# Second cross attention of a two-layer block: keys projected once per batch instead of folded into the queries

## What is computed

```python
def _L1_xattn_ref(q, k, v, Wq, bq, Wk, bk, Wv, bv, Wo, bo):
    HEADS = 16; D_MODEL = 128; D_K = D_MODEL // HEADS
    qh = (q @ Wq + bq).reshape(B, LQ, HEADS, D_K).transpose(0, 2, 1, 3)
    kh = (k @ Wk + bk).reshape(B, LKV, HEADS, D_K).transpose(0, 2, 1, 3)
    vh = (v @ Wv + bv).reshape(B, LKV, HEADS, D_K).transpose(0, 2, 1, 3)
    attn = jax.nn.softmax(jnp.einsum('bhqd,bhkd->bhqk', qh, kh) / np.sqrt(D_K), axis=-1)
    out = jnp.einsum('bhqk,bhkd->bhqd', attn, vh)
    return out.transpose(0, 2, 1, 3).reshape(B, LQ, D_MODEL) @ Wo + bo
```

## Time and profile before

| | |
|---|---|
| median of 3 runs | 667.15 us (667.14 to 670.14) |
| the profiled execution's own time | 664.66 us |
| its span in the profile | 662.9 us |
| TensorE clock granted | full, all through |
| busy share TensorE, VectorE, GpSimd, ScalarE | 94%, 75%, 57%, 53% |
| first cross attention, scores of batches | about 120 to 324 us |
| second cross attention, scores of batches | 428 to 627 us |

### The profile page before, as it was taken

One profiled execution on the slowest core, in us unless ns is written; L12 is line 12 of the kernel. 1 busy time (PEld: TensorE's weight loads), 2 busy tenths in 40 slices (PEclk: granted clock), 3 DMA queues, 4 the chain that ended last, 5 costly groups with the idle time before them and its releaser, 6 DMA issues.

```text
span 662.9 us, 19804 instructions
## 1 busy us (share of the span) xinstructions
PE 621.5 (94%) x8743; PEld 464.5 (70%) x8743; DVE 493.9 (75%) x796; ACT 353.0 (53%) x550; POOL 379.3 (57%) x272
## 2 busy tenths in 40 slices
PE   8889898899999999999898979999999999999997
PEld 4566785677777777777776556677777777777774
DVE  3666738799989889896665764877888988977543
ACT  2065663655646646647354316286586586664443
POOL 1362453388888888574220326078988988955400
PEclk9999999999999999999999999999999999999999
DMA  9600003000000002000032000001101100000000
GB/s 267 244 1 3 3 2 134 2 2 3 2 2 2 2 2 95 4 2 2 1 132 120 1 0 1 1 2 48 48 2 49 48 2 2 2 2 2 2 1 15
DMA packets 4657, 20.87 MB, mean 31 GB/s; under 512 B 500, under 2 KB 756, under 8 KB 4572
## 3 DMA queue, kind: packets, MB, share of 16 engines
q1 hardware_dynamic: 4572, 19.60, 8.8%
HBM read 19.37 MB, written 0.23 MB: 30 GB/s over the span
## 4 chain that ended last, share of the span: by engine, by line
PE 72%; DVE 12%; ACT 8%; issue 5%; POOL 2%; DMA 1%; POOLq 0%; DVEq 0%
PE psum L1125 18%; PE psum L1024 10%; PE psum L1066 5%; PE psum L1073 5%; PE psum L212 5%; PE psum L1068 5%; DVE scratch L1241 3%; PE psum L1003 3%; PE psum L1030 1%; PE psum L241 1%; PE psum L1042 1%; POOL scratch L626 1%; ACT scratch L1159 1%; ACT lv L286 1%; PE psum L1036 1%
## 5 line engine op out<-in xcount | busy, mean ns | idle before, releaser
L1226 POOL TENSOR_TENSOR scratch<-scratch 125x896 bf16<-125x896 f32 x136 | 238.5, 1765 | 117.7 <-ACT scratch L1206 117.5
L1206 ACT ACTIVATE scratch<-psum 125x896 f32<-125x896 f32 x192 | 173.1, 915 | 147.0 <-PE psum L1125 145.8
L1241 DVE TENSOR_REDUCE scratch<-psum 128x1 f32<-128x500 f32 x336 | 209.8, 671 | 14.1 <-PE psum L1024 6.4
L1125 PE MATMUL psum<-scratch 128*125 128x448 bf16 (+2 forms) x624 | 143.6, 355 | 0.5 <-ACT scratch L1206 0.2
L1066 PE MATMUL psum<-tok,scratch 125*128 125x65 bf16 x1344 | 108.9, 195 | 1.8 <-DVE kT L1286 1.8
L1068 PE MATMUL psum<-tok,scratch 125*128 125x64 bf16 x1344 | 108.3, 192 | 0.0
L1066 PEld LDWEIGHTS psum<-tok,scratch 125*128 125x128 bf16 x1344 | 95.3, 97 | 15.6 <-issue 2.6
L1024 PE MATMUL psum<-scratch 128*128 128x500 bf16 x273 | 102.3, 375 | 3.3 <-DVE scratch L1241 2.0
L1068 PEld LDWEIGHTS psum<-tok,scratch 125*128 125x128 bf16 x1344 | 90.2, 99 | 16.1
L1125 PEld LDWEIGHTS psum<-scratch 128*125 128x125 bf16 (+2 forms) x624 | 80.0, 136 | 26.1 <-ACT scratch L1206 0.8
L1226 DVE TENSOR_TENSOR scratch<-scratch 125x896 bf16<-125x896 f32 x56 | 68.6, 1227 | 18.1 <-ACT scratch L1206 17.0
(11 more groups left out here) (337 smaller groups left out, 896.7 us busy)
## 6 DMA issues: line engine op xcount, KB each, us to landing
nrm<-turned_dram SPq DMA_DIRECT2D x8, 750.0 KB, 4.6
raw<-ctx_dram SPq DMA_DIRECT2D x4, 672.0 KB
w_third<-fifth_dram SPq DMA_DIRECT2D x3, 636.0 KB, 5.4
w_third<-third_dram SPq DMA_DIRECT2D x2, 844.0 KB, 21.1
w_third<-third_dram SPq DMA_DIRECT2D x2, 843.5 KB, 19.2
w_fourth<-fourth_dram SPq DMA_DIRECT2D x3, 542.5 KB, 5.7
w_first<-first_dram SPq DMA_DIRECT2D x1, 996.0 KB, 4.8
w_second<-second_dram SPq DMA_DIRECT2D x1, 834.0 KB, 6.7
```

The source lines that it names most:

```text
L1125: mm = nc.tensor.matmul(bank(S + f, HALF, CP), lhs[0:rows, CP * c:CP * c + CP], rhs[0:rows, HALF * f:HALF * f + HALF], start=(rows == 128) ...
L1206: nc.scalar.activation(CR["p"][0:CP, n % RING, :].rearrange("p (f n) -> p f n", f=2), psum[0:CP, S:S + 2, 0:HALF], ACT.Exp).then_inc(self. ...
L1226: ops.tensor_tensor(CR["pl"][0:CP, n % RING, :], CR["p"][0:CP, n % RING, :], p_high(n % RING), ALU.subtract).then_inc(done, 1)
L1241: nc.vector.tensor_reduce(mxp[:, r, t:t + 1], bank(B, TB), X_AXIS, ALU.max).then_inc(self.aux_freed, 1)
```

## The change

- cross2's keys are made as such: K is a new unit, one float32 matmul of 500 context tokens against Wk (all 128 key features), three a batch. ScalarE writes its high part with the bias (`keys_act`), VectorE its low part (`keys_dve`), both in bf16.
- SP regroups them from there by transfers within SBUF into four groups of 4 heads (`keys_in`): per group the high, low and high rows, 32 each, and a row of ones. A batch takes 12 transfers for its first 1000 keys and 12 for the other 500.
- The queries are spread to the same rows by a constant (`spread`), 96 rows per group: high, high, low. With the row of the maximum the scores need 97 rows and one pass: four matmuls of 224 columns instead of four of 448.
- The maxima go over 96 rows of such groups, in 8 tiles of 112 query rows (24 maxima instead of 21).
- `keyed_placement` is the new order in cross2: Q in chunk 1, maxima from chunk 2 on, K in chunks 7 to 9 with two maxima each.
- In the last batch of cross1 the keys of batches 0 and 1 are made in chunks 0 to 2 and 8 to 10 (`EARLY_KEYS`); TensorE waits for their low parts ahead of chunk 3 and of the last sums.
- GpSimd has chunk 1's low part too in cross2; ScalarE makes the copies of N there; the query projection is one matmul in place of four, scaled per head group on ScalarE and VectorE.

```diff
+GROUPS, MAXIMA, QROWS = 4, 8, 112
+        def key_group(slot, g):
+            at = 4 * CTX // 2 * slot + CTX // 2 * g
+            return flat[:, at:at + CTX // 2].bitcast(BF16)
...
+        KEYED = [("Q", 0), ("Q", 1)] + [("M", u) for u in range(MAXIMA * TBLK)] + [("A", 0), ("A", 1)]
+        EARLY_KEYS = {CHUNKS * (BATCH - 1) + (0, 8)[kb] + t: (kb, t) for kb in range(2) for t in range(TBLK)}
+            if keyed:
+                return n % 2 == 0 if n >= CHUNKS * (BATCH - 1) + 3 else n % CHUNKS not in (0, 11)
+        def keyed_placement(front, outputs, keys):
+            at = [[] for _ in range(CHUNKS)]
+            maxima = iter(KEYED[2:2 + MAXIMA * TBLK])
+            def some(c, n):
+                at[c] += [[u] for u in itertools.islice(maxima, n)]
+            if front:
+                at[1] += [KEYED[0:2]]
+                some(2, 3)
+                some(3, 1)
+            if outputs:
+                at[3] += [[]] * (not front) + [[("N", 0)], [("N", 1)]]
+            if front:
+                some(3, 2)
+                for c in range(4, 11):
+                    some(c, 2 if c in (7, 8, 9) else 3)
+                at[11] += [[], [KEYED[-2]], [KEYED[-1]]]
+            if outputs:
+                at[5] += [[("O", 0)]]
+            if keys:
+                for t in range(TBLK):
+                    at[7 + t] += [[("K", t)]]
+            return at
...
+                elif u[0] == "K":
+                    eng.wait_ge(keys_low, TBLK * b + u[1] + 1)
...
+                    if self.keyed:
+                        for g in range(GROUPS):
+                            mm = nc.tensor.matmul(psum[0:96, self.home(idx + g // 2), 224 * (g % 2):224 * (g % 2) + 224],
+                                                  par("spread", 96 * g, 96 * g + 96), qT[:, :, 56 * b:56 * b + 56],
+                                                  start=True, stop=True)
+                elif kind == "M" and self.keyed:
+                    t, r = k // MAXIMA, k % MAXIMA
+                    if k == 0 and b:
+                        self.wait_freed(pe, self.index("Q", 1, b))
+                    elif k == 0:
+                        pe.wait_ge(self.front_low, 2)
+                    if r == 0 and t != 1:
+                        pe.wait_ge(keys_loaded[i][t // 2], 192 * (b // 2 + 1))
+                    mm = nc.tensor.matmul(bank(B, TB, QROWS), CR["qa", i][0:96, QROWS * r:QROWS * r + QROWS],
+                                          key_group(i, r // 2)[0:96, TB * t:TB * t + TB], start=True, stop=True)
+            def keys_pe(self, pe, b, t, B):
+                if b == 0:
+                    pe.wait_ge(loaded["keys"], 16)
+                pe.wait_ge(turned_loaded[t], 16 * (b + 1))
+                return nc.tensor.matmul(bank(B, TB), par("x_wk"), turned[:, TB * t:TB * t + TB],
+                                        start=True, stop=True)
+            def keys_act(self, act, b, t, B):
+                cols = slice(TB * t, TB * t + TB)
+                if b:
+                    act.wait_ge(keys_loaded[(b - 1) % 2][t // 2], 192 * ((b - 1) // 2 + 1))
+                nc.scalar.activation(key_high[:, cols], bank(B, TB), ACT.Identity, bias=col("x_bk")
+                                     ).then_inc(keys_high, 1)
+            def keys_dve(self, dve, b, t, B):
+                cols = slice(TB * t, TB * t + TB)
+                dve.wait_ge(keys_high, TBLK * b + t + 1)
+                nc.vector.scalar_tensor_tensor(key_low[:, cols], bank(B, TB), col("x_bk"), key_high[:, cols], ALU.add,
+                                               ALU.subtract).then_inc(keys_low, 1)
...
+                    if self is cross1 and n == CHUNKS * (BATCH - 1) + 3:
+                        pe.wait_ge(keys_low, TBLK)
...
+                    if self.keyed:
+                        if c == 0:
+                            self.wait_freed(pe, self.index("A", 1, b))
+                            pe.wait_ge(self.front_low, 2)
+                            pe.wait_ge(ones_loaded, 32)
+                        for g in range(GROUPS):
+                            mm = nc.tensor.matmul(psum[0:CP, S + g // 2, 224 * (g % 2):224 * (g % 2) + 224],
+                                                  key_group(i, g)[0:97, CP * c:CP * c + CP],
+                                                  CR["qa", i][0:97, 224 * g:224 * g + 224], start=True, stop=True)
...
+                    if self is cross1 and n in EARLY_KEYS:
+                        kb, t = EARLY_KEYS[n]
+                        if kb:
+                            self.wait_freed(pe, self.index("O", 0, BATCH - 2))
+                        cross2.keys_pe(pe, kb, t, SIDE[t]).then_inc(keys_made, 1)
+                if self is cross1:
+                    pe.wait_ge(keys_low, 2 * TBLK)
...
-                    if self.biased:
-                        nc.scalar.activation(CR["qb", i][96:97, cols], psum[64:65, B, 0:HALF], ACT.Copy)
-                    nc.scalar.activation(CR["qa", i][0:64, cols], bank(B, HALF, 64), ACT.Copy)
-                    ins = nc.scalar.activation(CR["qa", i][64:128, cols], bank(B, HALF, 64), ACT.Copy)
+                    ins = nc.scalar.activation(CR["qa", i][0:64, cols], bank(B, HALF, 64), ACT.Copy)
+                    if not self.keyed:
+                        ins = nc.scalar.activation(CR["qa", i][64:128, cols], bank(B, HALF, 64), ACT.Copy)
...
-                    if self is cross1 and b == BATCH - 1 and c in (2, 4, 6, 8):
-                        cross2.context_act(act, (c - 2) // 4, (c - 2) // 2 % 2)
-                    if self is cross2 and b < BATCH - 2 and c in (4, 6):
-                        self.context_act(act, b + 2, c // 2 - 2)
...
+            def keys_in(b, part):
+                cols = slice(2 * TB, CTX) if part else slice(0, 2 * TB)
+                for g in range(GROUPS):
+                    rows = slice(32 * g, 32 * g + 32)
+                    for k, keys in enumerate((key_high, key_low, key_high)):
+                        sp.dma_start(key_group(b % 2, g)[32 * k:32 * k + 32, cols], keys[rows, cols]
+                                     ).then_inc(keys_loaded[b % 2][part], 16)
...
+            for b in range(2, BATCH):
+                for t in range(TBLK):
+                    sp.wait_ge(keys_low, TBLK * b + t + 1)
+                    if b < BATCH - 1:
+                        turned_in(b + 1, t)
+                    if t:
+                        sp.wait_ge(cross2.scores, CHUNKS * (b - 2) + 4 * t + 4)
+                        keys_in(b, t - 1)
```

361 lines of the change are left out of this document (195 added, 166 removed).

## The result

The changed kernel takes 692.8 us (690.87 to 693.36), the kernel before 667.33 in the same comparison: ratio 1.0366, 95% interval 1.0332 to 1.040. I had said 674.5, with 663 to 685 as the range. The sign was right, the size was not: +25.5 us instead of +7.7. The profiled execution took 693.36 us, span 691.6, which is 28.7 more than the 662.9 of the span before. The two differences, 25.5 and 28.7, are not the same thing: the profiled execution before was the only one on record at a granted clock of 1.000 (664.66 us), while 28 others of that kernel, run beside the experiments, took 666.32 to 669.5 us at mean clocks of 0.989 to 0.996.

A forecast was written before the change was run, and what follows sets the result against it. TensorE, busy 94% of the span and 72% of the chain, was taken as the bound, plus a serial path between batches. Terms 8.5 - 1.7 - 4.1 + 0.9 + 4.1 = +7.7 us gave 674.5 us, range 663 to 685.

The forecast's parts named there:

- the first maximum at 5.3: Second attention, batches 1 to 5: first maximum 5.3 us after the batch's first scores, waiting for both query low parts.
- the serial end 2.05: Second attention, steady batch: serial path from last maximum to the next batch's first scores, 2.05 us, as before the change.
- TensorE idle some 1.9 us: Second attention, chunk 2: TensorE idles some 1.9 us before the first maximum, with that chunk's sums queued behind it.
- Chunks 7 to 9 ... 2.30 each. Sum 16.4.: Second attention, steady batch: chunks with a key unit take 2.30 us each; chunks 2 to 9 sum to 16.4.
- VectorE's idle time in chunks 7 to 9 covers its key parts: Second attention, chunks 7 to 9: the key parts on VectorE were costed at nothing.
- Eight issues took 3.91 us, 0.49 each: SP's queue: 0.49 us per transfer issue, used to price the key regrouping; 27 issues make 13.2 us a batch.
- it just hides: Second attention: the first regrouping lot takes 11.0 us, wanted by the next first maximum 11.4 later, so costs nothing.
- Rival 3: Regrouped keys land late and hold chunk 2's first maximum: +14 more, 688 us; chance 0.12.
- my +4.1: First cross attention's last batch, making the keys of two batches: +4.1 us, range +2.5 to +5.5.
- 2.4 for two chunks: Second attention's last batch: GpSimd's low part keeps two chunks from being shorter than 2.4 us; batch ends at 17.1, -4.1.
- Rivals 1 and 2: TensorE's sum decides, 660.4 us, chance 0.17; or a batch keeps its length, 666.5 us, chance 0.18.
- rival 1: Second attention: TensorE's work, 23.1 us a batch, decides; -1.1 a batch for seven, 660.4 us in all; chance 0.17.

The follow-up runs named there:

- the first three experiments: Against the changed kernel: sixteen constant matmuls ahead of the wait, 690.11 us; queries' low parts before the mean, 683.39; chunk 2's sums before the first maximum, 684.77.
- two buffers: Against the changed kernel: keys of odd and even batches get buffers of their own, batch 1's in memory the MLP uses later; 697.66 us, ratio 1.0452.

## Why the prediction was wrong

**The order of work held, and so did the sign.** The long wait in chunk 2 that ends with VectorE's query low part (1.78 us, said "some 1.9"), the first maximum at 5.3, the last key unit to the last maximum 3.4 (from 517.81 to 521.22), the serial end 2.05 (2.06), the score groups at 0.39 and the wait before chunk 3 of the first attention (1.54, said "1.6 to 2") came as written or nearly. On the scores, the case against the page "TensorE: Matmul & The Clock Gate" of the Trainium skill, section "LDWEIGHTS", stands: four pairs of load and matmul in 0.39 us leave no room for four loads of 104 ns one behind the other. My row for it had weights of 128 columns; these scores have the 125 in question.

**First failed step: the clock is in none of my terms.** "TensorE idle some 1.9 us" stands in the prediction as a price of 1.9. It costs 1.6 more in three batches of five, 4.8 us in all, and the first three experiments show that it goes when the wait is filled, shortened or cut. The granted clock of the profiled execution before was 1.00 throughout, and I took that as a constant of every row I read. The stretches at 328, 404, 438 and 680 add about 5 us more in the profiled execution (1.5, 0.9, 1.1 and 1.7). The first follows a wait of 2.48 us that the change made, though waits of up to 2.3 us at that place in other experiments had none behind them. That the others belong to the change was not shown: in the experiments they came and went where nothing was edited, and TensorE was busy in the records all through the 10 us ahead of 680, so a wait is not their only occasion. Nor is the kernel before free of them, by the clocks of 0.989 to 0.996 in its other executions. Some 3 of the 28.7 us are therefore a matter of which execution was profiled.

**Second: "Chunks 7 to 9 ... 2.30 each. Sum 16.4."** It was 17.4. Of the 1.0, chunks 7 to 9 have 0.8 (2.41, 2.65 and 2.64) and the chunks before them 0.2. The key unit's two records take 0.92 to 0.95 us, not 0.85, and a maximum 0.21 to 0.24, not 0.21, so that TensorE's own chunk is 2.41, as the run without the key part shows. On top the key part holds chunks 8 and 9 at 2.65. The sentence "VectorE's idle time in chunks 7 to 9 covers its key parts" is the error: VectorE does have the time, but it spends it in front of the key part, waiting for ScalarE, with the maxima queued behind; and the key unit's bank comes back only then. Over five batches the batch is 5.4 us longer than said. Batch 0, which is 0.45 longer rather than equal where no half clock stands in it, belongs here too.

**Third: "Eight issues took 3.91 us, 0.49 each"** was the wrong row for a transfer from one place of SBUF to another of 62.5 KB: 0.72 each. In the loop the conclusion "it just hides" still held, by 0.9 us (12 issues from 517.39 to 526.35, the last of them at 525.7 or so, 2.0 to land, wanted at 528.63). In the first attention, where two batches' keys follow each other in eight chunks, I had not asked at all. There the wait, with the half clock behind it, is the 2.8 missing: with two buffers, and no wait, the batch lasts 27.0, where my +4.1 meant 27.2. Rival 3 had the mechanism and the wrong place. The page "DMA: Bandwidth & Descriptors" of the Trainium skill, section "Bandwidth", has 0.95 us for 64 KB. That is the busy time of the DMA engines for a load from HBM issued by GpSimd, which is not the time of an issue on SP, so it could not replace the row; it lies as far above the 0.72 as my 0.49 lies below.

**Fourth: the last batch,** "2.4 for two chunks", assumed 1.68 us for GpSimd's low part and 1.09 for VectorE's. Side by side they took up to 2.05 and 1.62, and the batch 18.57 instead of 17.1. That the two slow each other had been in my own rows, where VectorE's low part is 1.76, and I used it only as a bound.

Rivals 1 and 2 did not occur. The run without key units shows where rival 1 had its point: the rest of the change does win about 1.0 us a batch, 1.4 with the sums of chunk 2 ahead. (Its TensorE work adds up to 22.96 us, not 23.1, which would have made it about 1 us faster still.)

**Open:** whether one long wait or much waiting brings the clock down; why it fell in every other batch; what brings the half clocks outside the loop, in both kernels; and whether a fourth side bank would free the key chunks, which was not tried, because the scores take four banks, the sums one and the side work the other three.

## What to carry over

An engine's idle time covers new work only if that work is ready when the idle time comes: in an order written out by hand, ask what stands behind the new instruction, and which bank it keeps. Price a new TensorE wait twice, once for itself and once at half clock behind it, and try first to cut it in two with work that is there anyway. Before you give an edit the credit for a shorter stretch, look how long that stretch is in the runs that leave it alone. When a step's period is set by a chain through three engines, moving one link (another bank, another place in the order) pays one side with the other; leave the link out once to see what it is worth before rearranging it.

## What the hardware did that I had not expected

The granted clock fell to 0.50 after a wait of 1.78 us in batches 1, 3 and 5 and not after the same wait in 2 and 4; with an edit in the last batch alone it was batches 2, 4 and 6. Each stretch lasted some 3.4 us and cost 1.6. Regrouping transfers of 62.5 KB took 0.66 to 0.75 us each to issue on SP in lots of twelve, another figure in every execution, and 2.0 us to land. Six low parts in a row on VectorE were 1.06 us apart, and 1.6 us long when GpSimd worked beside it.
